# Keeping the projected V of three head groups in on-chip buffers, and starting the next group's projection four steps later

## What is computed

```
x   = x + attn(layernorm(x), ctx)
q   = (x @ Wq + bq).reshape(1, B * N, H, hd)
kv  = (cond @ Wkv + bkv).reshape(1, -1, 2, H, hd)
q, k = _fq_sym(q * scale, axis=-1), _fq_sym(k, axis=-1)
v   = _fq_sym(v, axis=2)  # one scale per head and channel, over all context rows
attn = softmax(q @ k^T)
attn = _fq_unsigned(attn, axis=-1)
out = (attn @ v) @ Wp + bp
x   = x + ffn(layernorm(x))
```

## Time and profile before

| | us |
|---|---|
| median of 3 runs | 1953.9 (1947.21 to 1955.61) |
| the profiled execution's own time | 1951.71 |
| its span | 1949.8 |
| DVE busy | 1693.6 (87%) |
| PE busy | 1651.8 (85%) |
| POOL busy | 1449.2 (74%) |
| ACT busy | 1372.3 (70%) |
| DMA queue of SP, share of 16 engines | 80.7% |

### The profile page before, as it was taken

The page is one execution under the profiler, slowest core; times in us unless marked ns, Lnnn a source line. Parts: engine busy times, 40 slices in busy tenths (PEclk is TensorE's granted clock), DMA queues, the critical chain, the costliest instruction groups (busy, mean ns, idle before and its releaser), DMA issues.

```text
span 1949.8 us, 40601 instructions
## 1 busy us (share of the span) xinstructions
PE 1651.8 (85%) x16216; PEld 1126.0 (58%) x16216; DVE 1693.6 (87%) x2665; ACT 1372.3 (70%) x1324; POOL 1449.2 (74%) x1166
## 2 busy tenths in 40 slices
PE   7997888988788888887888888878978878689997
PEld 6874566665555666554566564434444545368875
DVE  6766999999879999997999999989989989976663
ACT  2444988888678888886888888677778868632221
POOL 1341788998898888988898898988998887733332
PEclk9998999998989999988999998566689989799998
DMA  5676999899989899999999998997978977732221
GB/s 179 211 207 158 197 196 198 190 197 182 216 166 192 183 200 183 190 196 193 197 190 186 202 175 167 200 166 137 179 153 168 208 160 141 165 94 46 60 55 44
DMA packets 861852, 327.97 MB, mean 168 GB/s; under 512 B 786081, under 2 KB 815841, under 8 KB 861537
## 3 DMA queue, kind: packets, MB, share of 16 engines
q1 hardware_dynamic: 861664, 325.38, 80.7%
HBM read 83.30 MB, written 48.63 MB: 68 GB/s over the span
## 4 chain that ended last, share of the span: by engine, by line
DVE 33%; PE 23%; POOL 16%; issue 14%; DMA 8%; ACT 5%; SPq 2%; POOLq 0%; DVEq 0%; ACTq 0%
DVE S L1141 29%; POOL PT L1384 11%; PE PS L764 5%; DMA PP<-Pr 5%; PE PS L660 4%; PE PK L815 3%; PE PK L600 3%; PE PS L627 2%; ACT Pr L967 2%; PE PO L679 1%; PE PK L602 1%; POOL VQ L1319 1%; POOL VB L1322 1%; PE PO L602 1%; SPq L544 1%
## 5 line engine op out<-in xcount | busy, mean ns | idle before, releaser
L1141 DVE TENSOR_SCALAR_CACHE_REDUCE S<-PS,SQN 128x1536 f32<-128x1536 f32 (+1 forms) x768 | 1286.6, 1713 | 97.8 <-PE PS L660 74.7
L967 ACT ACTIVATE Pr<-S,MS 128x5888 uint8<-128x5888 f32 x200 | 1041.5, 5207 | 239.3 <-DVE MJ L1163 151.3
L1384 POOL CAST PT<-PP 128x1536 uint16<-128x1536 uint8 (+1 forms) x800 | 1100.9, 1421 | 91.5 <-DMA PP<-Pr 90.5
L660 PE MATMUL PS<-KT,QT 96*128 96x512 bf16 (+1 forms) x2496 | 707.1, 408 | 136.4 <-DVE S L1141 124.1
L679 PEld LDWEIGHTS PO<-VI,PT 128*128 128x128 f16 x9200 | 347.4, 99 | 339.1 <-issue 136.4
L679 PE MATMUL PO<-VI,PT 128*128 128x32 bf16 x9200 | 365.4, 180 | 106.4 <-ACT AO L925 74.0
L660 PEld LDWEIGHTS PS<-KT,QT 96*128 96x128 bf16 (+1 forms) x2496 | 207.2, 104 | 344.8 <-issue 160.4
L600 PE MATMUL PK<-WG,CT 128*128 128x128 f32 (+1 forms) x1272 | 224.2, 307 | 14.4 <-DMA CT<-ctxt 9.2
L602 PE MATMUL PK<-CT,WG 128*128 128x128 f32 (+1 forms) x1272 | 212.0, 294 | 0.0
L600 PEld LDWEIGHTS PK<-WG,CT 128*128 128x128 f32 (+1 forms) x1272 | 175.7, 202 | 17.4 <-issue 12.6
L602 PEld LDWEIGHTS PK<-CT,WG 128*128 128x128 f32 x1272 | 166.5, 193 | 1.6 <-issue 0.3
(11 more groups left out here) (154 smaller groups left out, 1449.1 us busy)
## 6 DMA issues: line engine op xcount, KB each, us to landing
CT<-ctxt SPq DMA_DIRECT2D x180, 256.0 KB, 3.3
k_rows<-KS SPq DMA_DIRECT2D x44, 512.0 KB, 4.1
v_rows<-VS SPq DMA_DIRECT2D x33, 256.0 KB, 3.9
VQ<-v_rows SPq DMA_DIRECT2D x33, 256.0 KB, 3.8
q_rows<-QS SPq DMA_DIRECT2D x13, 512.0 KB, 4.1
W13F<-w13T SPq DMA_DIRECT2D x12, 352.0 KB, 3.9
PP<-Pr SPq DMA_TRANSPOSE x200, 6.1
XT<-x SPq DMA_DIRECT2D x12, 256.0 KB, 3.3
```

Source lines behind the costliest of these rows:

```text
L660: last = pe.matmul(PS[n % 2][p0:p0 + r, f:f + w], QT[h % 3][0:PARTS * HD, q0:q0 + r], KT[h % 3][0:PARTS * HD, c * CHUNK + f:c * CHUNK + f ...
L967: act.activation(Pr[i % 2].rearrange("p t q b -> p t b q"), S[i % 2].rearrange("p (t b q) -> p t b q", b=2, q=P), ACT.Exp, bias=MS[:, i % ...
L1141: v.tensor_scalar(S[i % 2][:, c * CHUNK:c * CHUNK + CW[c]], PS[n % 2][:, 0:CW[c]], neg_step, None, ALU.mult, ALU.min, accum_out=MN[:, i % ...
L1384: gp.tensor_copy(PT[i % 2][:, 2 * t0:2 * t1, :].rearrange("p (t b) q -> p t b q", b=2), PP[i % 2][:, t0:t1, :].bitcast(U8).rearrange("p t ...
```

## The change

VS, VQ and the DRAM tensor for V are gone. There is one buffer VV per batch, twelve in all; ACT writes V of a unit there, DVE reads its maximum there, and POOL scales it in place once the scale is known, then rounds it into VB as before. Seven of the twelve buffers lie in memory that is used by the output rows (OL, XR, XO, OT) later on, so the load of BP into one of those waits until the last V is scaled and moves from step 140 to 153. ACT waits, ahead of the first unit of a batch, for the previous group's batch in that buffer to be scaled. POOL scales a batch every 2/3 of a step, 1.5 in a step in place of 2, and SP turns them at that pace, beginning 5 steps behind the group's last unit as before. Groups 2 and 3 begin 7 instead of 3 steps behind the last unit of the one before: group 2 in steps 43 to 88, group 3 in 95 to 140. The even heads' Q and K come two steps later in a pair.

```diff
-ODD_HEAD_AT, EVEN_HEAD_AT = [1, 3, 5, 6, 8], [13, 14, 16, 18, 20]
+ODD_HEAD_AT, EVEN_HEAD_AT = [1, 3, 5, 6, 8], [15, 16, 18, 20, 22]
...
-BP_AT = WP_AT - 6
+BP_AT = WP_AT + 7
...
-        start = steps[g, NU - 1] + 3
+        start = steps[g, NU - 1] + 7
...
-        VS = ring("VS", 2, [NB * P], F32)
+        VV = ring("VV", 2, [NB * P], F32)
...
-        VQ = ring("VQ", 3, [NB * P], F32)
+        VV += [tmp(f"VV{b}", [NB * P], F32) for b in range(2, 5)]
...
+            VV += [tmp(f"VV{b}", [len(BATCH[b]) * P - (P - ULAST) * (b == NBT - 1)], F32, early) for b in range(5, NBT)]
...
-        v_loads = {}
+        v_turns = {}
         for g in range(1, NG):
             for b in range(NBT):
-                v_loads.setdefault(STEP_OF_UNIT[g, NU - 1] + 4 + b // 2, []).append((g, b))
+                v_turns.setdefault(STEP_OF_UNIT[g, NU - 1] + 5 + b * 2 // 3, []).append((g, b))
...
-                for g, b in dve_batches.get(i, []):
-                    store_v(g, b)
...
-                for g, b in v_loads.get(i, []):
-                    load_v(g, b)
...
                 if i == BP_AT:
+                    sp.wait_ge(M["s_vg"], (NG - 1) * NBT)
...
-                for g, b in v_loads.get(i - 1, []):
+                for g, b in v_turns.get(i, []):
                     turn_v(g, b)
...
-                    if kb >= NBT + 2:
-                        act.wait_ge(M[f"s_vd{kb % 2}"], 16 * stored_v(kb - 2))
+                    if g >= 2:
+                        act.wait_ge(M["s_vg"], (g - 2) * NBT + u // NB + 1)
...
-                v_to = VS[kb % 2][:, u % NB * P:u % NB * P + n] if g else VF[:, u * P:u * P + n]
+                v_to = VV[u // NB][:, u % NB * P:u % NB * P + n] if g else VF[:, u * P:u * P + n]
...
-                link(v.memset(VS[a], 0.0))
...
-                gp.wait_ge(s_vq[k % 3], 16 * ((k - NBT) // 3 + 1))
...
-                             (end + 4.95 + b // 2, v_quant, (g, b))]
+                             (end + 4.95 + b * 2 / 3, v_quant, (g, b))]
...
-            todo += [(WP_AT + 10.15 + part, bias_parts, (part,)) for part in range(5)]
+            todo += [(WP_AT + 8.15 + part, bias_parts, (part,)) for part in range(5)]
```

More of the change, by code:

```diff
@@ L138, in link, with build @@
         self.sync()
-def build(nc, x, ctxt, ctxl, Wq, bq, Wkv, bkv, Wp, bp, w13T, w2T, norm_w, eye, Qd, Kd, Vd, Od, Rd, out):
+def build(nc, x, ctxt, ctxl, Wq, bq, Wkv, bkv, Wp, bp, w13T, w2T, norm_w, eye, Qd, Kd, Od, Rd, out):
     ctx = ExitStack()
@@ L218, in build @@
         with ExitStack() as early:
+            VV += [tmp(f"VV{b}", [len(BATCH[b]) * P - (P - ULAST) * (b == NBT - 1)], F32, early) for b in range(5, NBT)]
+        with ExitStack() as early:
             OL = ring("OL", 2, [DONE_CH], F32, early)
@@ L231, in build @@
         OT3 = tmp("OT3", [P], F32)
+        tmp("PADA", [16], F32)
         AO = tmp("AO", [NT, 2, 2 * HD], F32)
@@ L267, in build @@
         names = """cst s_x0 s_x1 s_w s_sd s_xn s_tp s_tpe s_q s_qe s_qs s_qd0 s_qd1 s_wg s_wg1 s_bk s_b3 s_bv s_ku s_kve
-                   s_kr s_kn s_ki s_kc s_k6 s_k8 s_kh s_kd s_kl s_kp s_vd0 s_vd1 s_vr s_v8 s_vt s_vg s_vi s_wp s_q0 s_ao s_qk s_ev s_mx s_exp s_pad s_pvp s_pv s_pve s_rz
+                   s_kr s_kn s_ki s_kc s_k6 s_k8 s_kh s_kd s_kl s_kp s_vr s_v8 s_vt s_vg s_vi s_wp s_q0 s_ao s_qk s_ev s_mx s_exp s_pad s_pvp s_pv s_pve s_rz
                    s_nrm s_nr0 s_un s_ao0 s_ao1 s_dve s_act s_pool
@@ L278, in build @@
         s_vb = [sem(f"s_vb{r}") for r in range(VRING)]
-        s_vq = [sem(f"s_vq{r}") for r in range(3)]
         block = ctx.enter_context(nc.Block())
@@ L305, in last_of_step @@
             return a * NU + b
-        def stored_v(kb):
-            return (kb - NBT) // 2 + 1
         dve_batches = {}
@@ L331, in load_unit @@
                 sp.dma_start(CT[k % RING][:, :, 0:n], ctxl if u == NU - 1 else ctxt[u]).then_inc(s_ct[k % RING], 16)
[L333 to L338, removed]
             def store_k(g, b):
@@ L355, in load_wg @@
                 sp.dma_start(WG[:, :, 1, :], wkv_v[:, :, C + g * GC:C + (g + 1) * GC]).then_inc(M["s_wg1"], 16)
[L357 to L364, removed]
             def turn_v(g, b):
@@ L1057, in batch @@
                 yield
-                vals = VS[kb % 2][:, 0:w] if g else VF[:, us[0] * P:us[0] * P + w]
+                vals = VV[b][:, 0:w] if g else VF[:, us[0] * P:us[0] * P + w]
                 chain.mark(v.tensor_reduce(VMX[:, g % 2, b:b + 1], vals, X, ALU.max, apply_absolute_value=True))
@@ L1314, in v_quant @@
                 w = (len(us) - 1) * P + unit_rows(us[-1])
-                q = VQ[k % 3][:, 0:w]
+                q = VV[b][:, 0:w]
                 if b == 0:
                     gp.wait_ge(M["s_vr"], g + 1)
-                gp.wait_ge(s_vq[k % 3], 16 * ((k - NBT) // 3 + 1))
                 link(gp.tensor_scalar(q, q, VS3[:, g % 2, 2:3], MAGIC, ALU.mult, ALU.add))
@@ L1467 @@
         nc.dram_tensor("k_rows", (NG, KEYS, GH, P), BF16, kind="Internal").ap(),
-        nc.dram_tensor("v_rows", (NG - 1, P, KP), F32, kind="Internal").ap(),
         nc.dram_tensor("attn_out", (NT * P, C), F32, kind="Internal").ap(),
```

## The result

The changed kernel takes 1928.12 us (median of 6 runs, 1917.13 to 1932.28) against 1948.91 of the kernel before (6 runs, 1947.21 to 1955.61): a ratio of 0.9879, 95% interval 0.9849 to 0.9908. It is faster by 1.2%. The forecast was 1922, 6 us lower, inside the range of 1906 to 1940. It started from 1953.9, the median of the first three of those six runs. The gain itself was put at 30 us; it is 20.8 between the medians and 23.1 between the profiled executions.

The account below looks back on a forecast made before the run. DVE was taken to bound the kernel except in three V-reload stretches, 41.5 us over pace; 41.5 - (5 + 5 + 3) = 28.5, plus 1.5 relief, gives 30 us off 1951.71: 1921.7, said as 1922, range 1906 to 1940.

Parts of the forecast that it names:

- the three stretches: Steps 40 to 50, 88 to 97, 135 to 145, where V is reloaded, scaled and turned: 41.5 us over their pace.
- The left-over of groups 1 and 2: Excess staying in these groups' V stretches after the change, from queue and POOL: 5 us each.
- the signs: Profile after: no V reload or POOL wait for it, V stretches 7.3 to 7.9 us a step, ACT's P wait 40 to 55.
- The price of a load: Queue time of one 256 KB V reload on SP's queue: 0.81 us taken, bounds 0.81 to 1.38.
- 8.1 against 7.44 us per step: POOL's unpacking plus V's scaling in a V step: 8.1 us at two batches, 7.44 at 1.5.
- 3 for group 3: Excess staying in group 3's V stretch, which has no CT loads: 3 us.
- at nothing: Small things, among them BP's load 13 steps later with bias_parts needing it one step later: no cost.
- The relief of 1.5 us: Thinner queue shortens ACT's waits for PP outside the three stretches: 1.5 us gained, bounds 0 and 3.
- A: SP's V turns stand ahead of P's while POOL's batch is late: 15 to 30 us lost; chance 0.15 for 1930 to 1943.
- C: Each pair's last K piece, issued two steps later, arrives late: 2 us a pair, 14 for seven, 1936; chance 0.07.
- D: Nothing comes of it, DMA being so full that what the reload leaves fills again: 1945 to 1954; chance 0.06.
- B: PE's low clock holds on after six light steps, about 4.5 us over 7.26 a step: 1962 or more; chance 0.06.

Follow-up runs that it names:

- e6: Changed kernel plus 36 unneeded 256 KB DRAM-to-DRAM copies at the places of V's reload, without stores: 1946.79 us, 0.9981 of the kernel before.
- e9: Changed kernel plus the same 36 unneeded copies, moved to where V's stores stood: 1931.02 us, 0.9898 of the kernel before.
- e5: Changed kernel with the 36 stores of V put back and no loads: 1928.54 us, 0.9891 of the kernel before.
- e8: The changed kernel itself, measured once more: 1926.90 us, 0.9866 of the kernel before.
- e3: Changed kernel with V scaled and turned two batches a step: 1927.72 us, 0.9867 of the kernel before.
- e1: Kernel before with the new schedule alone, V's stores and reload kept: 1959.92 us, 1.0026 of the kernel before.
- e2: Changed kernel with 36 stores of V and 36 unneeded DRAM-to-DRAM copies in place of the reload: 1956.31 us, 1.0003 of the kernel before.
- e7: Changed kernel with V one step earlier and the next group's projection starting 5 instead of 7 steps later: 1931.79 us, 0.9903 of the kernel before.
- e11: e7 with BP's load and the bias also 4 steps earlier: 1928.42 us, 0.9892 of the kernel before.

## Why the prediction was right or wrong

**Right: where the gain is and what makes it.** It was put in the three stretches, through the queue, and e6 against e9 shows that: the same bytes cost 16.2 us more there than where DVE sets the pace, where no cost can be told. That the stores are worth nothing that can be told by themselves is e5. The left-over of groups 1 and 2 was put at 5 + 5 us and is 7.1 + 3.5, in e8 4.3 + 3.8. Of the signs, the steps 41 to 50, 93 to 102 and 145 to 154 take 7.82, 7.51 and 7.27 us each (7.3 to 7.9 forecast), and ACT's wait for P is 57.5 us (40 to 55 forecast). That the time came as near as 6 us is in part luck: the gain fell short by a third from median to median (31.9 forecast, 20.8 measured), and the fuller median before came out 5 us lower.

**The price of a load** was taken as 0.81 us, with bounds of 0.81 to 1.38. Measured in time, for a copy, it is (0.9981 - 0.9866) x 1950.7 / 34.5 = 0.65 us (by the prediction's count, 11.5 loads to a group), with an interval of 0.19 either way (the half widths 0.0021 and 0.0026 put together as roots of squares). So of the bounds the lower one agrees with it and the upper doesn't. The 2.0 us that the prediction estimated from the Trainium skill (DMA: Bandwidth & Descriptors, section Bandwidth) is a time of moving, not a price; beside full traffic the copy costs the kernel a third of it, and the measurement decides.

**Right outcome, wrong working: POOL.** The reasoning by 8.1 against 7.44 us per step, and by POOL's wait for the reload, isn't borne out: two batches a step are as fast within some 7 us (e3), and e1's 30.0 us of waits cost between nothing and 10 us (e1 against e2). POOL's order showed its price where other work joined the unpacks, in group 3 and in e7's step 81.

**The step that failed: "3 for group 3", with the bias priced "at nothing".** The sum took V's scaling in group 3 as POOL's only extra work. The bias's pieces moved as well, from steps 156 to 160 to steps 154 to 158, where they share a step with the last two pieces of WP (steps 154 and 155) and with a pair's normalisation (step 155); the kernel before had them behind these. The prediction looked at the bias only for when its load comes and when its result is read. Measured: 6.9 us of excess (7.8 in e8). Of after's 6.9, 1.5 lie in steps 145 to 152, where V is scaled, and 5.3 in steps 153 to 160. With the pieces of WP and the bias thinned the whole is 3.3, which is what V alone had been given. That V lies just ahead of them isn't the main cause, since in e7, with V done in step 147, steps 153 to 160 still take 60.1 us. That the bias's new place is the cause is what is left, and fits; no run moved the bias back alone, and in e11, where it stands in steps 150 to 154, it meets WP's pieces too.

**The relief of 1.5 us** outside the stretches wasn't seen: after lost 2.3 there, e8 gained 0.8. Two profiled executions of the same kernel differ by 4.7 us over the steps (1478.77 and 1474.12), so a term of this size can't be decided here. From the profiled execution the gap to the forecast is 30 - 23.1 = 6.9 us: 3.9 of group 3, 0.6 of groups 1 and 2, 3.8 from the relief and the losses elsewhere, less 1.4 ahead of and behind the steps.

**The rivals.** A, SP's turn waiting for POOL's batch: 2.1 us in the run against 15 to 30. C, K late: no wait of PE for KT. D, nothing comes of it: the ratio's interval excludes it. B, the low clock holding on: the windows of the kernel after for steps 41 to 43, where the projection comes back in step 42, and for step 48:

```profile
489.11:496.13 7.02, 6.53 (x65) 3.25 (x62) 6.82 (x10) 5.41 (x4) 6.89 (x7) 0.50 1.06 250
496.13:504.66 8.53, 8.44 (x92) 6.18 (x89) 7.51 (x11) 5.92 (x5) 8.37 (x9) 0.79 0.97 171
504.66:510.98 6.32, 5.62 (x72) 3.79 (x70) 6.29 (x11) 5.81 (x6) 6.24 (x7) 1.00 0.97 186
...
542.48:552.79 10.31, 10.31 (x83) 6.19 (x80) 7.08 (x10) 5.79 (x5) 10.31 (x9) 0.50 0.84 174
```

After six light steps at 0.50 the clock is back within the step in which the projection returns, as in the earlier trace rows; that step costs 1.3 us more than the pace, not 4.5 for several steps. The 4.5 was too high besides: PE is busy 6.26 us in an ordinary step, and 6.26 + 4.8 is 3.8 over 7.26; step 48, at 0.50 throughout, is 3.05 over. By the Trainium skill (TensorE: Matmul & The Clock Gate, Part 1) activity releases the throttle, and the trace agrees: 0.50, 0.79, 1.00. But a price of the clock stands in the left-over itself: step 48 takes 10.31 us at 0.50, and in e8's execution 6.86 at 1.00. These 3.45 us are more than the 2.83 by which the two executions differ over group 1's stretch (86.99 and 84.16). The prediction had worked out its 5 us from the queue and POOL alone. Whether a late P made PE stand and the clock fall there, or the clock fell by itself and made P late, no run separates.

## What to carry to other kernels

Price a removed transfer by what ends the step at its place, not by its size alone: the same 36 copies cost 16 us more where P's turning was the late one than where DVE was the limit. When work is moved, list everything that its engine does in the new steps, the untouched pieces too, and add it up per step. When a schedule moves, move the stretch that you measure with it. Profile the same kernel twice before a difference of a few us is given a cause.

## What the runs showed of the hardware

A single step inside a busy stretch can fall to the lower clock. On PE's timeline of the kernel after, before and in step 48 (the last column is the idle time ahead):

```profile
537.09 0.69 PE L581 MATMUL PK<-CT,WG 128*128 128x128 f32 x4
...
540.87 1.49 PE L639 MATMUL PS<-KT,QT 96*64 96x512 bf16 x6 [0.97 <-DVE S L1119]
...
542.63 1.20 PE L579 MATMUL PK<-WG,CT 128*128 128x128 f32 x4
```

PE had stood twice for DVE's evictions, the second time 0.97 us, and from there the same projection takes 1.20 us in place of 0.69. The granted clock is 0.50, the lower of its two levels (1.2 GHz), for the whole of step 48. The stand alone doesn't explain it: in e8's step 79 PE stands as long for an eviction, and the scores behind it run at the higher level.

```profile
783.59 0.81 PE L639 MATMUL PS<-KT,QT 96*128 96x512 bf16 x3 [0.97 <-DVE S L1119]
```

In e8's execution step 48 takes 6.86 us. Step 134 takes 9.27 us at 0.69 in the one and 6.79 at 1.00 in the other, where step 133 takes 8.49 at 0.67. So which steps dip changes from one execution to the next. That this makes the scatter of 15 us between runs of the changed kernel is only argued, and it isn't all of it: step 0 begins at 184.78 us in one execution and at 191.88 in the other.

The DMA share was no guide to what a transfer costs: it reads 1.00 both in e6 and in e9, 7.5 us apart over the same eleven steps.
